# A six-layer perceiver kernel: the next layer's weights and contexts loaded one layer earlier, the norms' roots moved in front of the layer boundary, the result stored in four parts

## The reference

```
x += xattn_0(norm(x), ctx, mask)      # one head, its own norm of the result
x += delta_rule(norm(x))              # q, k, v with short convolutions, chunked delta rule, FIR mix
x += experts_0(norm(x))               # softmax router, 2 of 8 experts
x += xattn_1(norm(x), ctx)            # 16 heads of 16
x += self_attention(norm(x))          # 16 query heads, 4 key heads, rope
x += experts_1(norm(x))               # 16 routed experts and 4 shared ones
```

## Time and profile before

| | |
|---|---|
| runs | 1928.67 us median, 1927.96 to 1937.13 |
| profiled execution | 1936.78 us, of which the span of instructions is 1935.0 us |
| PE busy | 1617.6 us (84%) |
| PEld busy | 1229.5 us (64%) |
| DVE busy | 1229.2 us (64%) |
| ACT busy | 772.5 us (40%) |
| POOL busy | 605.8 us (31%) |
| HBM read, written | 166.49 MB, 47.25 MB, 110 GB/s over the span |
| transfers | 216.40 MB in 145226 packets |

### The profile page before, as it was taken

The page is one execution under the profiler, slowest core; times in us unless marked ns, Lnnn a source line. Parts: engine busy times, 40 slices in busy tenths (PEclk is TensorE's granted clock), DMA queues, the critical chain, the costliest instruction groups (busy, mean ns, idle before and its releaser), DMA issues. The chain is left out here.

```text
span 1935.0 us, 40824 instructions
## 1 busy us (share of the span) xinstructions
PE 1617.6 (84%) x16490; PEld 1229.5 (64%) x16490; DVE 1229.2 (64%) x2383; ACT 772.5 (40%) x1711; POOL 605.8 (31%) x438
## 2 busy tenths in 40 slices
PE   6885879899988689999985889999578588689997
PEld 3443357555665589999984645555466477379996
DVE  4566779670283556766623167777569677767886
ACT  1222742121233243444332447777134322346664
POOL 2330000000010377777523035555156332303200
PEclk9987979999899889999998879999789789789999
DMA  8882049401124455566478814444100000101001
GB/s 271 285 269 63 0 130 212 125 22 18 49 104 125 158 201 193 197 217 204 151 167 187 240 58 155 155 149 143 58 1 1 2 4 4 44 1 39 23 6 45
DMA packets 145226, 216.40 MB, mean 112 GB/s; under 512 B 38608, under 2 KB 118544, under 8 KB 139152
## 3 DMA queue, kind: packets, MB, share of 16 engines
q1 hardware_dynamic: 105296, 102.74, 18.0%
q10 hardware_dynamic: 29376, 52.57, 9.3%
q0 software_dynamic: 10368, 58.47, 9.3%
HBM read 166.49 MB, written 47.25 MB: 110 GB/s over the span
## 5 line engine op out<-in xcount | busy, mean ns | idle before, releaser
L2129 POOL TENSOR_TENSOR a_pr<-a_pr,a_inv 128x1028 f32<-128x1028 f32 x64 | 121.7, 1901 | 101.0 <-DVE a_inv L2237 101.0
L1972 DVE TENSOR_TENSOR f_hL<-f_hr,f_hH 128x512 fp32r<-128x512 f32 x92 | 85.0, 961 | 100.7 <-ACT f_hH L1922 100.6
L1484 POOL TENSOR_TENSOR b0m_pm<-b_dr,b_gates 128x256 f32<-128x256 f32 x16 | 13.3, 831 | 404.4 <-SPq L1449 378.0
L92 PE MATMUL ps<-f_xTH,f_w1H 128*128 128x256 f32 x368 | 107.9, 293 | 24.2 <-issue 23.6
L2216 ACT ACTIVATE a_pr<-ps,a_neg 128x257 f32<-128x257 f32 x256 | 118.2, 475 | 10.4 <-DVE a_neg L2263 5.9
L92 PE MATMUL ps<-g_w1H,g_hH 128*128 128x256 f32 x320 | 92.4, 289 | 17.0 <-DVE g_hL L2889 16.2
L93 PE MATMUL ps<-f_xTL,f_w1H 128*128 128x256 f32 x368 | 106.1, 288 | 0.0
L94 PE MATMUL ps<-f_xTH,f_w1L 128*128 128x256 f32 x368 | 106.0, 288 | 0.0
L2905 DVE SCALAR_TENSOR_TENSOR x<-ps,g_gate,x 128x256 f32<-128x256 f32 x256 | 105.6, 476 | 0.0
L92 PE MATMUL ps<-f_w2H,f_hH 128*128 128x256 f32 x368 | 104.1, 283 | 0.0
L93 PE MATMUL ps<-f_w2L,f_hH 128*128 128x256 f32 x368 | 104.1, 283 | 0.0
(11 more groups left out here) (425 smaller groups left out, 4788.7 us busy)
## 6 DMA issues: line engine op xcount, KB each, us to landing
a_kv<-kv SPq DMA_DIRECT2D x64, 513.0 KB, 3.5
a_ctxT<-in_ctxT SPq DMA_DIRECT2D x32, 514.0 KB, 6.9
a_ctxR<-in_ctx SPq DMA_DIRECT2D x32, 512.0 KB
kv<-b_kv ACTq DMA_DIRECT2D x31, 513.0 KB
b_kvctx<-in_ctxT ACTq DMA_DIRECT2D x31, 257.0 KB, 3.4
kv<-f_raw ACTq DMA_DIRECT2D x15, 513.0 KB, 11.4
outs<-f_yo SPq DMA_DIRECT2D x23, 256.0 KB, 2.1
kv<-f0r_kv ACTq DMA_DIRECT2D x9, 513.0 KB, 5.8
```

The source lines that it names most:

```text
L92: e.matmul(out, wh, xh, start=start, stop=False)
L1972: e.tensor_tensor(h[1][:, j % 2, 2 * q:2 * q + 2, :], hr[:, q, :, :], h[0][:, j % 2, 2 * q:2 * q + 2, :].bitcast(F32), ALU.subtract).then_ ...
L2129: e.tensor_tensor(pr[:, b % 3, :, :], pr[:, b % 3, :, :], inv[:, b % 2, :].unsqueeze(2).to_broadcast([P, HG, NK]), ALU.mult).then_inc(*p_p ...
```

## The change

- **Weights of layer two.** A new class `DeltaWeights` holds the weights and convolution taps; SP issues their loads at the end of its list in the first layer.
- **One `KeysAhead` for all layers**, allocated from the other end of SBUF and kept until the fourth layer, with three context slots. Weights and the first three contexts are loaded once, by SP in the first layer; `host` gives each block its count, PSUM banks and output slots. The load of context b+3 goes on over the blocks' ends, so the last contexts of a block's batches have been loaded in the block in front.
- **Fewer units in front of the first transpose**: one in place of three in the delta rule (the other two after tile 15, ahead of `project(1)`), two in place of four in the router (nine in place of seven after the last transpose), two in place of five in the fourth layer (nine in place of six behind).
- **Roots**: DVE's three steps and ACT's root stand at the end of the layer in front.
- **Router weights**: PE waits for them at the first logits, no longer ahead of the first transpose.
- **Self attention's weights**: a new class `SelfWeights`. SP issues the loads in the fourth layer's loop (when batch 8 is weighed), and POOL does all the work in 20 pieces, three in every four batches from batch 17 on, each behind that batch's L2129. The block `sw` goes.
- **First experts, end**: keys' weights and contexts no longer lie in `raw1` and `raw2`; the gathered rows do (`yg` is a part of `raw2`), so POOL waits for the last `v_w2` ahead of them.
- **Store**: SP of the last layer stores each group of 512 rows when its last result is added; the block `store` goes.

```diff
-    def dve(self, e):
-        K = self.K
-        e.wait_ge(*self.aggr.at(NT))
-        e.tensor_scalar(K.std[:, :], K.mv[:, :, 1], 1e-5, None, ALU.add).then_inc(*self.var.up())
-        e.wait_ge(*self.root.at(1))
-        e.reciprocal(K.rstd[:, :], K.std[:, :]).then_inc(*self.inv.up())
-        e.wait_ge(*self.inv.at(1))
+            e.wait_ge(*self.aggr.at(NT))
+            e.tensor_scalar(K.std[:, :], K.mv[:, :, 1], 1e-5, None, ALU.add).then_inc(*self.var.up())
+            e.wait_ge(*self.root.at(1))
+            e.reciprocal(K.rstd[:, :], K.std[:, :]).then_inc(*self.inv.up())
+            e.wait_ge(*self.inv.at(1))
 ...
-    def __init__(self, Y, first, count, banks, ctx, kv, w, bk):
-        self.K, self.first, self.count, self.banks = Y.K, first, count, banks
-        self.ctx, self.kv, self.w, self.bk = ctx, kv, w, bk
+    SLOTS = 3
+
+    def __init__(self, Y):
+        self.K, self.Y = Y.K, Y
+        self.w, self.bk = Y.sb("w", [P, 2, DC, D]), Y.sb("bk", [P, DC])
+        self.ctx = places(Y.sb("ctx", [P, self.SLOTS, DC, NK]))
         self.ld_w = Y.sig("dma", "wkv")
-        self.ld_c, self.st = ([Y.sig("dma", f"{n}{s}") for s in range(len(places))] for n, places in (("kvctx", ctx), ("kv", kv)))
+        self.ld_c = [Y.sig("dma", f"kvctx{s}") for s in range(self.SLOTS)]
         self.mm, self.ev = Y.sig("pe", "kv"), Y.sig("act", "kv")
-        self.formed = self.taken = 0
+        self.formed = self.taken = self.first = self.last = 0
 ...
+    def host(self, Y, count, banks, kv):
+
+        self.first, self.last = self.last, self.last + 3 * count
+        self.banks, self.kv = banks, kv
+        self.st = [Y.sig("dma", f"kv{s}") for s in range(len(kv))]
 ...
+        for b in range(self.SLOTS):
             self.load(e, b)
 ...
+                if b + self.SLOTS < B:
+                    self.load(e, b + self.SLOTS)
 ...
-def store(K):
-    with Layer(K, "out") as Y:
-        stored = Y.sig("dma", "out")
-        with K.nc.Block() as block:
-            @block.sync
-            def _(e):
-                e.dma_start(K.out.rearrange("(t p) d -> p t d", p=P), K.x[:, :, :]).then_inc(*stored.up(16))
-                e.wait_ge(*stored.at(16))
 ...
+                K.front.load(e)
+                K.keys.begin(e)
 ...
+                K.norms["b0"].act(e)
 ...
+    def load(self, e):
+        I = self.K.ins
+        for j, n in enumerate("qkv"):
+            e.dma_start(self.wqkv[:, j, :, :], features(I["L0_attn_W_" + n])).then_inc(*self.loaded.up(16))
+        e.dma_start(self.conv[:, :, :, :], I["L0_attn_conv"]).then_inc(*self.loaded.up(16))
 ...
-                    A.pe(e, 3)
+                    A.pe(e, 1)
                     A.wait_taken(e)
-                    e.wait_ge(*ld_b.at(16))
                     for t in range(8):
                         turn(t)
-                    e.wait_ge(*ld_1.at(80))
+                    e.wait_ge(*ld_1.at(64))
                     project(0)
                     for t in range(8, NT):
                         turn(t)
+                    e.wait_ge(*a_xnT.at(NT))
+                    A.pe(e, 2)
+                    A.wait_taken(e)
                     project(1)
 ...
-                    A.begin(e)
-                    N.act(e)
-                    A.act(e, 3)
+                    A.act(e, 1)
 ...
+                                if n == 6:
+                                    A.act(e, 2)
+                                    e.wait_ge(*ld_f.at(16))
 ...
+                K.norms["f0"].act(e)
 ...
-                    e.wait_ge(*ld_r.at(16))
-                    A.pe(e, 4)
-                    T.pe(e, lambda t: A.pe(e, (t + 1) % 2))
-                    A.pe(e, 7)
+                    A.pe(e, 2)
+                    T.pe(e, lambda t: A.pe(e, (t + 1) % 2), ld_r.at(16))
+                    A.pe(e, 9)
                     e.wait_ge(*v_ch.at(2))
 ...
                     e.wait_ge(*st_y[s].at(16 * ((BLOCKS - s + 1) // 2)))
+                e.wait_ge(*v_w2.at(BLOCKS))
 ...
-                        e.wait_ge(*v_w2.at(BLOCKS))
-                        A.begin(e)
 ...
+                K.norms["a1"].act(e)
 ...
-                    A.pe(e, 5)
+                    A.pe(e, 2)
                     T.pe(e, lambda t: A.pe(e, 1))
 ...
-                    A.pe(e, 3 * AHEAD[3] - 21)
+                    A.pe(e, 3 * AHEAD[3] - 18)
 ...
+                    if done == LB:
+                        K.next.load(e)
 ...
+                    if b >= 2 * LB and b % BT:
+                        K.next.piece(e, (b - 2 * LB) // BT * (BT - 1) + b % BT - 1)
 ...
+    def load(self, e):
+        I = self.K.ins
+        e.dma_start(self.w[:, :, :], features(I["L1_attn_WqkvT"])).then_inc(*self.ld_w.up(16))
+        e.dma_start(self.rope[:, :, :], I["rope"]).then_inc(*self.ld.up(16))
+        for n, x in enumerate("qk"):
+            e.dma_start(self.nw[:, n, :], I[f"L1_attn_{x}_norm_w"].partition_broadcast(P)).then_inc(*self.ld.up(16))
+
+    def piece(self, e, n):
+        halves = [slice(0, 32), slice(32, 64)]
+        if n < 12:
+            m = n % 6
+            at = (slice(0, P), m // 3, cols(m % 3, 512))
+            if n == 0:
+                e.wait_ge(*self.ld_w.at(16))
+            if n < 6:
+                e.tensor_copy(self.ws[0][at], self.w[at]).then_inc(*self.hi.up())
+            else:
+                e.wait_ge(*self.hi.at(m + 1))
+                e.tensor_tensor(self.ws[1][at], self.w[at], self.ws[0][at].bitcast(F32), ALU.subtract)
+        elif n < 15:
+            lo, hi = ((0, 8), (8, self.HQ), (self.HQ, self.HT))[n - 12]
+            k, heads = lo // self.HQ, [P, hi - lo, self.W]
+            if n == 12:
+                e.wait_ge(*self.ld.at(48))
+            e.tensor_tensor(self.cw[:, lo:hi, :], self.rope[:, 0:1, :].to_broadcast(heads),
+                            self.nw[:, k:k + 1, :].to_broadcast(heads), ALU.mult)
+        elif n < 19:
+            k, half = divmod(n - 15, 2)
+            lo, hi = ((0, self.HQ), (self.HQ, self.HT))[k]
+            a, b, part = halves[half], halves[1 - half], [P, hi - lo, 32]
+            e.tensor_tensor(self.sw[:, lo:hi, a], self.rope[:, 1:2, a].to_broadcast(part),
+                            self.nw[:, k:k + 1, b].to_broadcast(part), ALU.mult)
+        elif n == 19:
+            e.memset(self.eps[:, :], 1e-6)
 ...
-                    @block.gpsimd
-                    def _(e):
-                        e.memset(eps[:, :], 1e-6)
-                        e.wait_ge(*ld_w.at(16))
-                        for c in range(DC):
-                            e.tensor_copy(ws[0][:, c, :], w[:, c, :]).then_inc(*p_hi.up())
-
-                    @block.vector
-                    def _(e):
-                        N.dve(e)
-                        e.wait_ge(*ld.at(48))
-                        for n, (lo, hi) in enumerate(((0, HQ), (HQ, HT))):
-                            heads = [P, hi - lo, W]
-                            e.tensor_tensor(cw[:, lo:hi, :], rope[:, 0:1, :].to_broadcast(heads),
-                                            nw[:, n:n + 1, :].to_broadcast(heads), ALU.mult)
-                            for a, b in (half, half[::-1]):
-                                part = [P, hi - lo, 32]
-                                e.tensor_tensor(sw[:, lo:hi, a], rope[:, 1:2, a].to_broadcast(part),
-                                                nw[:, n:n + 1, b].to_broadcast(part), ALU.mult)
-                        for c in range(DC):
-                            e.wait_ge(*p_hi.at(c + 1))
-                            e.tensor_tensor(ws[1][:, c, :], w[:, c, :], ws[0][:, c, :].bitcast(F32), ALU.subtract)
 ...
+                out = K.out.rearrange("(t p) d -> p t d", p=P)
+                for g in range(NG):
+                    e.wait_ge(*v_y.at(outputs_of(len(jobs) - NG + g)))
+                    e.dma_start(out[:, cols(g, 4), :], K.x[:, cols(g, 4), :]).then_inc(*stored.up(16))
+                e.wait_ge(*stored.at(16 * NG))
```

164 lines of the change are left out of this document (80 added, 84 removed).

## The result

The changed kernel took 1911.14 us (median of 4 runs, 1900.92 to 1920.14) beside 1932.18 us for the kernel before on the same chip: ratio 0.9895, 95% interval 0.9848 to 0.9941. Two later comparisons with five rounds each gave 0.9884 (0.9842 to 0.9926) and 0.9859 (0.9825 to 0.9893). The gain is about 1.2 per cent, 23 us, where 43 were forecast, and 1911 lies outside the forecast's 1875 to 1900.

What follows compares the result with a forecast made beforehand. PE, 84% busy, was taken to set the time, with four waits at layer starts to remove. Six terms (7.7 + 6.7 + 5.1 + 15.4 + 2.9 + 5.0 = 42.8) took 1928.67 to 1885.9 us; forecast's own range 1880 to 1893, with rivals 1875 to 1900.

Steps and rivals of the forecast that it cites:

- A: Start of layer two: first transpose 11.4 us earlier, two units returning ahead of `project(1)` taken at 3.7; −7.7 (6.5 to 9).
- E: Start of the last layer: table and root earlier, bias awaited later, −1.9; shorter pause saves slow records, −1.0; −2.9 (1.9 to 3.5).
- D: Start of the self attention: loading, splitting and tables leave the boundary, POOL's pieces in the loop taken 0; −15.4 (8.5 to 17.5).
- B: Start of the experts: boundary −9.4 us, two more units behind the last transpose +2.7; −6.7 (6 to 7.5).
- the store: End of the kernel: three quarters stored earlier leave 1.6 us of transfer; −5.0 (4.5 to 5.3).
- The four waits: PE's waits at starts of layers, 24.6, 19.3, 17.1 and 6.8 us, for a transfer or POOL; the change targets these.
- C: Start of the second cross attention: boundary −10.6, three later units +3.5, contexts at the experts' end +2; −5.1 (3 to 7.5).
- Rival one: At A, B and C only the earlier normalizing counts: 8.2 us instead of 19.5, total 1897; chance 0.12.
- Rival three: POOL's pieces stretch the fourth layer's loop, by contention with DVE: 1937, chance 0.03; mild form 1896 to 1906, chance 0.03.
- rival four: Next layer's contexts sit behind stores, or first units still wait at A, B or C: 1892 to 1903; chance 0.05.
- Rival two: PE keeps its clock through shorter pauses and contexts fit free windows: C +2 +1.9, D +2, A +1: 1879; chance 0.09.

Runs made afterwards that it cites:

- The fill: Changed kernel plus eight identity transposes ahead of PE's wait for DVE in each tile of the self attention's first stage: stage 128.4 us instead of 135.7, ratio 0.9863.

## Why the prediction was wrong

The terms add up to 42.8 us and the stages gained 27.3. Of the 15.5 that are missing, the self attention's first stage has 5.5, the loop 4.8, A 4.7 and E 1.3; the other stages' deviations from the forecast nearly cancel.

**Right.** D's boundary (−15.4), B (−7.2 for −6.7), the store (−4.5 for −5.0). The four waits of the earlier trace rows were the right place. C is right in its sum (−4.4 for −5.1) by errors that cancel: the boundary gave 1.2 more than its 10.6, the way behind it cost 3.8 more than its 3.5, of which 2.5 are waits for ACT's way out that no term had, and the 2 us for the experts' end came out as 0.2. Rival one is out: B and C kept most of what PE gained, and in A, where −3.0 is near its 2.3, moving the units gave the rest back. Rival three is out too, and rival four's waits at A, B and C didn't come.

**The step that failed in D: that nothing in the loop waits for the weights.** The sum spread their 7 us of transfer over a loop "in which nothing waits for them before batch 17". True, and beside the point: PE's instructions are transfers too. With the one transfer of 1.5 MB on its way these stayed away for 9.2 to 10.6 us, PE stopped once for 0.8 to 2.4, and in six of eight profiles the granted clock fell behind it: +4.8 in the loop, of which 4.5 is lost clock in that window. Cut in six, the load costs nothing that can be seen (241.6, the length of the loop without load and pieces at the same clock at its start). The size is uncertain, since the loop's own start varies too: a kernel without load and pieces in it had 245.8.

**A, a term mis-sized.** −3.0 for −7.7. Two units in front of `project(1)` were costed at 3.7, with 1.18 for each, the price at the higher clock. From the second group's first transpose to `project(1)` it is 12.2 to 12.4 us in the three profiles after, for 6.0 before: 6.3 for the two units, which ran mostly at the lower clock (0.63). The block from the first transpose on grew by 7.4 (76.4 to 83.8); the last 1.1 isn't traced. The first transpose came 10.3 earlier for the forecast 11.4. Moving all units out of the way returned 6 to 7.

**The self attention's first stage**, +5.5 for 0, the largest single miss. The earlier trace rows end at the boundary; the 128 us behind them were read from one profile, which had the better of two rhythms. The changed kernel always showed the other. The sum had no term for it: it put the stage at nothing without a reason. The fill shows that the clock's falls carry it; why the change falls into this rhythm stays open.

**E**, −1.6 for −2.9: the granted clock fell in a pause of 3.2 as in one of 4.8, so the 1.0 for it was wrong. Rival two, which counted on the clock at C, D and E, is out: the units at 1044.72 and the transposes at 1613.68 ran at the lower clock, and D gave its 15.4 and no more.

The range was drawn around the sum of the terms' own bounds (which add up to 30.4 to 50.3, not 30 to 52). It had no room for the stages in between changing by themselves: a single stage varies by 3 to 8 us from execution to execution (in the table, of the same kernel before: loop 240.0 to 243.6, first stage 127.8 to 135.4). None of the prediction's three signs of being wrong came true on the mean: the loop grew by 4.8 (sign: more than 6), the end of the experts by 0.2 (more than 4), B's part behind its first transpose by 2.0 (more than two units of 1.2). No sign watched A or the self attention's first stage.

## What to carry to other kernels

A boundary is worth what the timeline says, but only if what is put elsewhere costs nothing there: a prefetch must be cut so small that the running loop's own transfers, the matmul engine's instructions among them, never stand behind it for long, and filler work belongs into a pause that is read off the trace, not in front of the stage that sets the pace. Where PE waits 2 to 3 us for another engine in every iteration, a few idle transposes ahead of that wait are worth trying, and before reading a stage's length off one profile, take a second.

## What the runs showed of the hardware

- The matmul engine's instructions come by DMA (q8, 16 KB a packet, one in 3.5 to 7.6 us in the loop). Behind one transfer of 1.5 MB the next packet came 9.2 to 10.6 us after the last, and the engine stopped for 0.8 to 2.4 us with no semaphore to show for it; with six transfers of 256 KB it didn't.
- The same stage with the same instructions has two stable rhythms, 128 and 135.5 us. In it the granted clock stayed at 1.00 with pauses of 0.8 to 1.75 us; behind pauses of 2.7 it was at its lower level (1.2 of 2.4 GHz) in every second case.
- After the stop of 1.85 us in the loop (1168.87 to 1170.72) the granted clock stayed at 0.50 from 1173 to 1189 although PE was busy without a break.
- POOL's 128x512 subtraction took 1269 to 1279 ns in the loop, for 1278 to 2114 in the last layer. The loop's DVE work beside it didn't lengthen it:

```profile
L2352 POOL TENSOR_TENSOR sqw_wL<-sqr_w,sqw_wH x6: 1269/1272/1279, 1204.9 to 1226.1; 128x512 fp32r<-128x512 f32 x6
```
